# First attention: scores formed twice, the second time keys by queries, with the exponential taken straight from PSUM

## The chip, the cores and the metric

The kernel runs on one core of a Trainium2 chip. The metric is the device time of one execution in microseconds (us), the median of several runs.

## What is computed

A batch of 16 sequences of 256 tokens, 256 wide, passes two transformer-like layers. The change is in the second step, a causal attention of the normed tokens over a context, with 16 heads of 16 channels and a mask over the keys:

```python
scores = jnp.einsum('bhqd,bhkd->bhqk', q, k) * scale
causal = jnp.tril(jnp.ones((Lq, Ls), bool))
full_mask = causal[None, None] & (mask[:, None, None, :] > 0)
scores = jnp.where(full_mask, scores, -jnp.inf)
p = jax.nn.softmax(scores, axis=-1)
return jnp.einsum('bhqk,bhkd->bhqd', p, v)
```

Around it stand the projections of query, key, value and output, each with a bias, and the addition of the result to x. The stages before it (a decaying sum) and after it (experts, time and channel mixing, a second attention, a last projection) are not touched.

## The kernel before

The whole x lies in SBUF. Each stage is a block with one program for each engine; a barrier parts the stages. In `causal_attention` (tiles named `xa_...`) every engine runs through `for b in long_turns(...)`: 16 batches and two turns of drain. The order on each engine is written out by hand and the engines meet at semaphores. The work of a batch is 16 units (query tile `t` of 128 queries, pair of heads), in four steps of four units.

- TensorE: `scores` (L692) multiplies queries by keys. A head pair stands on one quarter of the array's rows (32 of 128), so that eight products go to four PSUM banks from four quarters. `turn_unit` (L704) transposes the f32 probabilities through the full array into `p_p`. `sum_units` (L723) multiplies them by the values, on quarters of the array's columns (128 rows by 32 columns), with a column of ones that gives the sums. Projections (L654, L662) and the transposes of x, o and sums (L647, L732) use the full array. So three shapes of the array occur: full (128x128), row quarters (32x128), column quarters (128x32).
- VectorE: `shift_unit` (L940) reads scores from PSUM, adds the causal and key mask `neg`, writes `sc` and gives the minimum (the scores have their sign turned) to `nmax`. `copy_unit` (L949) copies half of the transposed units out of PSUM.
- ScalarE: `exponentials` (L860) forms `pr` from `sc` with `nmax` as its bias, one instruction for each head; `copy_unit` (L839) copies the other half; it also reads all projections out of PSUM.
- GpSimd: builds `neg` from the mask (L593, L596), `root`, `finish_values`, `add`.

For the first query tile only the first 128 keys are formed (`keys(t)`), for the second all 256.

## Time and profile before

| | |
|---|---|
| median of three runs | 1957.56 us (1953.01 to 1961.42) |
| span of the profiled execution | 1955.9 us |
| this stage, first scores to last addition | 90.9 to 408.2 us |
| TensorE busy over the span | 87% |
| VectorE, ScalarE, GpSimd busy over the span | 62%, 58%, 32% |

The profiled execution is shown with its span alone, 1955.9 us from first to last instruction, 1.7 us below the median. A matmul's row gives its start and a modelled end; rows that follow one another on TensorE overlap by the pipeline's depth, so what a matmul costs is read from start to start.

### The profile page before, as it was taken

Reading aid. Unit: us, or ns where it says so; the run is one execution under the profiler, and the core shown is the slowest. Engines: PE = TensorE matmul, PEld = TensorE weight load, DVE = VectorE, ACT = ScalarE, POOL = GpSimd, SP = SyncE. Lnnn points to the kernel's source line nnn. Section 1 sums busy time; section 2 is a strip of 40 time slices with the busy share of each in tenths; the row PEclk is TensorE's granted clock in tenths of the full one; section 3 lists DMA queues with packets and bytes.
Section 4 is the critical chain, followed back from the end, with each engine's and each line's share of the span. In section 5 each row is a group of like instructions: output and inputs, shape, how many; then the busy total and the mean of one; then the engine's idle time right before and its main releaser. Section 6 shows DMA issues by size and latency. Waiting matters only on the chain. (4 is left out here: it accounts for less than half of the span.)

```text
span 1955.9 us, 40754 instructions
## 1 busy us (share of the span) xinstructions
PE 1699.3 (87%) x13412; PEld 1389.0 (71%) x13412; DVE 1214.7 (62%) x4180; ACT 1133.1 (58%) x2600; POOL 621.2 (32%) x783
## 2 busy tenths in 40 slices
PE   6677777779999999999988999999996999999963
PEld 5555555557788888889976877777774777777742
DVE  6699999858211111101118899899954988888756
ACT  5599999932222222222326665666643888888855
POOL 4523333230211111101114566666622122222217
PEclk9899999979999999999988999999997999999985
DMA  3100010035855556557944000000002111111002
GB/s 119 48 26 26 19 26 18 3 103 187 272 182 182 194 165 205 166 188 243 324 156 150 22 22 23 22 18 16 22 1 73 35 34 34 34 34 35 2 1 86
DMA packets 111695, 171.96 MB, mean 88 GB/s; under 512 B 6832, under 2 KB 86576, under 8 KB 110864
## 3 DMA queue, kind: packets, MB, share of 16 engines
q1 hardware_dynamic: 95248, 142.55, 22.1%
q0 software_dynamic: 6480, 17.70, 3.1%
q10 hardware_dynamic: 9776, 9.31, 1.4%
q8 instruction: 101, 1.65, 0.3%
q14 instruction: 90, 0.74, 0.1%
HBM read 143.45 MB, written 26.08 MB: 87 GB/s over the span
## 5 line engine op out<-in xcount | busy, mean ns | idle before, releaser
L1909 ACT ACTIVATE moe_hT<-moe_p_h,lane_a 128x256 f32<-128x256 f32 (+1 forms) x344 | 131.4, 433 | 370.1 <-PE moe_p_h L1851 370.1
L1851 PE MATMUL moe_p_h<-moe_gT,moe_w 128*128 128x256 f32 (+1 forms) x1376 | 254.0, 343 | 0.8 <-issue 0.8
L1861 PE MATMUL moe_p_y<-moe_w,moe_hT 128*128 128x256 f32 x1136 | 252.3, 379 | 0.0
L1359 ACT ACTIVATE xb_pr<-xb_sc,xb_nmax 128x256 f32<-128x256 f32 x512 | 221.1, 501 | 39.3 <-DVE xb_nmax L1416 39.1
L1851 PEld LDWEIGHTS moe_p_h<-moe_gT,moe_w 128*128 128x128 f32 x1376 | 226.1, 191 | 24.9 <-issue 1.0
L1861 PEld LDWEIGHTS moe_p_y<-moe_w,moe_hT 128*128 128x128 f32 x1136 | 212.5, 190 | 27.1
L1416 DVE CUSTOM_DVE_ANT_0 xb_sc<-xb_p_s,xb_neg 128x256 f32<-128x256 f32 x512 | 187.1, 420 | 54.6 <-PE xb_p_s L1225 53.2
L860 ACT ACTIVATE xa_pr<-xa_sc,xa_nmax 128x256 f32<-128x256 f32 (+1 forms) x512 | 204.1, 453 | 17.6 <-DVE xa_nmax L940 17.1
L1741 POOL DMA_INDIRECT moe_gx<-moe_tokens,moe_source_i x71 | 67.3, 948 | 454.5 <-PE moe_p_t L1838 398.5
L2054 DVE TENSOR_TENSOR moe_gy<-moe_p_y,lane_a 128x256 f32<-128x256 f32 x71 | 27.5, 421 | 229.1 <-PE moe_p_y L1861 229.1
L2029 DVE COPY moe_gT<-moe_p_t 128x512 f32<-128x512 f32 (+1 forms) x43 | 25.7, 598 | 230.2 <-PE moe_p_t L1838 230.2
L1237 PE MATMUL xb_p_p<-ident,xb_pr 128*128 128x128 f32 x1024 | 145.3, 280 | 24.9 <-DVE xb_prT L1425 17.1
L940 DVE CUSTOM_DVE_ANT_0 xa_sc<-xa_p_s,xa_neg 128x256 f32<-128x256 f32 (+1 forms) x512 | 151.6, 352 | 10.7 <-PE xa_p_s L692 9.2
L1237 PEld LDWEIGHTS xb_p_p<-ident,xb_pr 128*128 128x128 f32 x1024 | 112.6, 142 | 52.9 <-ACT xb_pr L1359 27.1
L704 PE MATMUL xa_p_p<-ident,xa_pr 128*128 128x128 f32 x768 | 118.6, 283 | 20.8 <-DVE xa_prT L949 14.9
L2334 PE MATMUL mix_p_kv<-mix_fv,mix_hid_sq 128*128 128x256 f32 x512 | 115.7, 379 | 1.7 <-ACT mix_hid_sq L2543 1.7
L704 PEld LDWEIGHTS xa_p_p<-ident,xa_pr 128*128 128x128 f32 x768 | 84.5, 144 | 44.8 <-ACT xa_pr L860 24.1
L2411 PE MATMUL mix_p_h<-mix_mixed,mix_fk 128*128 128x256 f32 x512 | 114.5, 382 | 0.0
L2411 PEld LDWEIGHTS mix_p_h<-mix_mixed,mix_fk 128*128 128x128 f32 x512 | 98.6, 193 | 13.8
L2334 PEld LDWEIGHTS mix_p_kv<-mix_fv,mix_hid_sq 128*128 128x128 f32 x512 | 96.0, 190 | 14.5 <-ACT mix_hid_sq L2543 2.1
L1425 DVE COPY xb_prT<-xb_p_p 128x512 f32<-128x512 f32 x128 | 87.7, 685 | 1.7 <-PE xb_p_p L1237 1.6
L1341 ACT ACTIVATE xb_prT<-xb_p_p 128x512 f32<-128x512 f32 x128 | 74.8, 584 | 16.0 <-PE xb_p_p L1237 15.9
(344 smaller groups left out, 3447.2 us busy)
## 6 DMA issues: line engine op xcount, KB each, us to landing
moe_w<-in_L_ffn_w_dram SPq DMA_DIRECT2D x86, 1024.0 KB, 8.0
moe_rows_out<-moe_gy ACTq DMA_DIRECT2D x28, 256.0 KB, 7.1
xb_kv<-moe_w SPq DMA_DIRECT2D x18, 256.0 KB, 2.9
X<-in_x_dram SPq DMA_DIRECT2D x4, 1024.0 KB, 9.5
xa_ctx<-in_ctx_turned_dram SPq DMA_DIRECT2D x16, 256.0 KB, 2.8
moe_tokens<-moe_XN_s SPq DMA_DIRECT2D x16, 256.0 KB, 2.2
xb_k_in<-xb_kv SPq DMA_DIRECT2D x16, 256.0 KB, 2.6
xb_v_in<-xb_kv SPq DMA_DIRECT2D x16, 256.0 KB, 3.0
```

Source lines behind the costliest of these rows:

```text
L704: last = pe.transpose(p_p[m % 2][:, (e * TB + kt) * P:(e * TB + kt + 1) * P], pr[:, m % RB, e, kt * P:(kt + 1) * P], ident[:, :])
L860: last = act.activation(pr[:, n % RB, e, 0:width], sc[:, n % RB, e, 0:width], ACT.Exp, bias=nmax[:, n % RB, e:e + 1], scale=-1.0)
L940: last = dve.tensor_tensor_reduce(out=sc[:, n % RB, e, 0:keys(t)], in0=scored_in(n, e), in1=neg[:, s, t, 0:keys(t)], scale=1.0, scalar=3e3 ...
L1237: last = pe.transpose(p_p[m % 2][:, (e * TB + kt) * P:(e * TB + kt + 1) * P], pr[:, m % RB, e, kt * P:(kt + 1) * P], ident[:, :])
L1359: last = act.activation(pr[:, n % RB, e, :], sc[:, n % RB, e, :], ACT.Exp, bias=nmax[:, n % RB, e:e + 1], scale=-1.0)
L1416: last = dve.tensor_tensor_reduce(out=sc[:, n % RB, e, :], in0=scored_in(n, e), in1=neg[:, s, t, :], scale=1.0, scalar=3e38, op0=ALU.add, ...
L1425: dve.tensor_copy(*turned_unit(m)).then_inc(s_["p_copied_v"], 1)
L1851: last = pe.matmul(p_h[n % 3][:, k * width:(k + 1) * width], w1[:, r, ic, (2 * n + k) * P:(2 * n + k + 1) * P], gT[:, r % 2, ic, 0:width], ...
L1861: last = pe.matmul(p_y[:, t * D:(t + 1) * D], hT[:, hc, t * P:(t + 1) * P], w2[:, r, hc, :], start=(hc == 0), stop=(hc == HC - 1))
L1909: last = act.activation(hT[:, 2 * n + k, 0:width], p_h[n % 3][:, k * width:(k + 1) * width], ACT.Gelu, bias=b1[:, bass.ds(e * HC + 2 * n + ...
L2334: last = pe.matmul(p_kv[:, t * D:(t + 1) * D], hid_sq[:, hc, t * P:(t + 1) * P], fv[:, hc, :], start=(hc == 0), stop=(hc == HC - 1))
L2411: last = pe.matmul(p_h[m % 2][:, k * S:(k + 1) * S], fk[:, ic, (2 * m + k) * P:(2 * m + k + 1) * P], mixed2[:, 0, ic, :], start=(ic == 0), ...
```

## The change

The scores are formed twice. In the first pass (`score`, 12 fills of a bank for each batch, f = 0 to 11) queries stand on the partitions; TensorE first adds the mask itself (the identity times `off`, with `OFF` a power of two), then two or four products of row quarters on top of it in the same bank. VectorE only takes the minimum of the bank (`find_max`). GpSimd splits the minima into three bf16 parts that sum to them (`part`), TensorE transposes these (`turn_max`) and ScalarE copies them (`read_max`). In the second pass, one batch later (`cross`, g = 0 to 11), keys stand on the partitions: product of keys and queries, plus a product that adds the three parts of the minima (`pick` by `nmaxT`), plus the identity times `ahead`, the causal triangle. ScalarE takes the exponential of a whole bank of 512 out of PSUM (`exponentials`), with the key mask as its bias. These probabilities are already laid out for `sum_values`: the transposes of `turn_unit` and both copies of `copy_unit` are gone. The key bias of `finish_keys` moves from VectorE to ScalarE, the key mask `mask_keys` from GpSimd to VectorE; a transposed copy of the mask is one more small input.

```diff
-OFF = 1e30
+OFF = 2.0 ** 100
...
+FILLS = 12
+RING_S = 2
+RING_T = 3
+PARTS = 3
+SLOT = 16
...
+            def part(n):
+
+                slots = [parts[:, :, :, SLOT:].rearrange("p t o (u x) -> p t o u x", x=SLOT)[:, :, :, :, i] for i in range(PARTS)]
+                own = nmax[:, n % 2, :, :, :]
+                wait_alone(pool, s_["stood_p"], (s_["maxed"], FILLS * n + FILLS))
+                if n >= 1:
+                    wait_alone(pool, s_["stood_p"], (s_["turned_max"], n))
+                pool.tensor_copy(slots[0], own).then_inc(s_["split"], 1)
+                wait_alone(pool, s_["stood_p"], (s_["split"], 3 * n + 1))
+                pool.tensor_tensor(rest[:, :, :, :], own, slots[0], ALU.subtract).then_inc(s_["split"], 1)
+                wait_alone(pool, s_["stood_p"], (s_["split"], 3 * n + 2))
+                pool.tensor_copy(slots[1], rest[:, :, :, :]).then_inc(s_["split"], 1)
+                wait_alone(pool, s_["stood_p"], (s_["split"], 3 * n + 3))
+                pool.tensor_tensor(slots[2], rest[:, :, :, :], slots[1], ALU.subtract).then_inc(s_["parted"], 1)
...
+            def score(n, f):
+                if f == 0:
+                    pe.wait_ge(s_["q_ready"], n + 1)
+                    pe.wait_ge(s_["k_ready"], n + 1)
+                    pe.wait_ge(s_["diag_ready"], n + 1)
+                if FILLS * n + f >= RING_S:
+                    pe.wait_ge(s_["maxed"], FILLS * n + f - RING_S + 1)
+                bank, view = p_s[f % RING_S], fill_view(f)
+                if f < 8:
+                    c, r = divmod(f, 4)
+                    pe.matmul(view, ident_d[:, :], off[:, n % 2, 1:TB + 1, :].rearrange("p t n -> p (t n)").unsqueeze(1).broadcast_to([P, 2, S]),
+                              start=True, stop=False)
+                    for odd in range(2):
+                        last = pe.matmul(bank[:, odd * S:(odd + 1) * S], q[quad(r), n % 3, odd, c, P:2 * P], k[quad(r), n % 3, c, :],
+                                         start=False, stop=(odd == 1))
+                else:
+                    r = f - 8
+                    pe.matmul(bank[:, :].rearrange("p (m n) -> p m n", m=4), ident_d[:, :], off[:, n % 2, 0:1, :].broadcast_to([P, 4, P]),
+                              start=True, stop=False)
+                    for c in range(DC):
+                        for odd in range(2):
+                            last = pe.matmul(bank[:, (2 * c + odd) * P:(2 * c + odd + 1) * P], q[quad(r), n % 3, odd, c, 0:P], k[quad(r), n % 3, c, 0:P],
+                                             start=False, stop=(c == DC - 1 and odd == 1))
+                last.then_inc(s_["scored"], 1)
+
+            def cross(n, g):
+                if g == 0:
+                    pe.wait_ge(s_["max_ready"], n + 1)
+                if FILLS * n + g >= RING_T:
+                    pe.wait_ge(s_["exped"], FILLS * n + g - RING_T + 1)
+                bank, r = p_x[g % RING_T], g % 4
+                if g < 4:
+                    for c in range(DC):
+                        pe.matmul(bank[:, c * S:(c + 1) * S].rearrange("p (o n) -> p o n", o=2), k[quad(r), n % 3, c, P:2 * P], q[quad(r), n % 3, :, c, P:2 * P],
+                                  start=True, stop=False)
+                        pe.matmul(bank[:, c * S:(c + 1) * S].rearrange("p (o n) -> p o n", o=2), pick[quad(r), c, :], nmaxT[quad(r), :, P:2 * P],
+                                  start=False, stop=False)
+                        last = pe.matmul(bank[:, c * S:(c + 1) * S].rearrange("p (o n) -> p o n", o=2), ident_d[:, :], ahead[:, :].unsqueeze(1).broadcast_to([P, 2, P]),
+                                         start=False, stop=True)
+                else:
+                    c = g // 4 - 1
+                    pe.matmul(bank[:, :].rearrange("p (o n) -> p o n", o=2), k[quad(r), n % 3, c, 0:P], q[quad(r), n % 3, :, c, :], start=True, stop=False)
+                    pe.matmul(bank[:, :].rearrange("p (o n) -> p o n", o=2), pick[quad(r), c, :], nmaxT[quad(r), :, :], start=False, stop=False)
+                    last = pe.matmul(bank[:, :].rearrange("p (o n) -> p o n", o=2)[:, :, 0:P], ident_d[:, :], ahead[:, :].unsqueeze(1).broadcast_to([P, 2, P]),
+                                     start=False, stop=True)
+                last.then_inc(s_["crossed"], 1)
...
+            def sum_values(n, c):
+
+                pe.wait_ge(s_["exped"], FILLS * n + 8 + 4 * c)
+                if c == 0:
+                    pe.wait_ge(s_["v_ready"], n + 1)
+                if n > 0 or c > 0:
+                    pe.wait_ge(s_["sums_read"], DC * n + c)
+                for odd in range(2):
+                    for r in range(4):
+                        pe.matmul(p_o[quad(r), odd * S:(odd + 1) * S], v[:, n % 3, 0, head(c, r, odd), :], pr0[:, c, r, odd, :],
+                                  start=True, stop=False)
+                    for r in range(4):
+                        last = pe.matmul(p_o[quad(r), odd * S + P:(odd + 1) * S], v[:, n % 3, 1, head(c, r, odd), :], pr1[:, r, c, odd, :],
+                                         start=False, stop=True)
+                last.then_inc(s_["pv"], 1)
...
+            def turn_max(n):
+
+                pe.wait_ge(s_["parted"], n + 1)
+                for odd in range(2):
+                    for t in range(TB):
+                        last = pe.transpose(p_d[0][:, odd * S + t * P:odd * S + (t + 1) * P],
+                                            parts[:, t, odd, SLOT - 4 * odd:SLOT - 4 * odd + P], ident_d[:, :])
+                last.then_inc(s_["turned_max"], 1)
...
+            for b in range(B + 2):
+                here, past, old = b < B, 1 <= b <= B, b >= 2
+                if here:
+                    score(b, 0)
+                    score(b, 1)
+                if old:
+                    pe.wait_ge(s_["o_ready"], DC * (b - 2) + 1)
+                    turn_sums(b - 2, 1)
+                if past:
+                    if here:
+                        pe.wait_ge(s_["v_read"], b + 1)
+                    else:
+                        pe.wait_ge(s_["y_read"], B - 2)
+                    turn_max(b - 1)
+                if here:
+                    score(b, 2)
+                if b + 1 < B:
+                    if old:
+                        pe.wait_ge(s_["o_ready"], DC * (b - 1))
+                    else:
+                        pe.wait_ge(s_["q_read"], b + 1)
+                    project_keys(b + 1)
+                if here:
+                    score(b, 3)
+                if past:
+                    cross(b - 1, 0)
+                    cross(b - 1, 1)
...
+            def exponentials(n, g):
+
+                act.wait_ge(s_["crossed"], FILLS * n + g + 1)
+                if n >= 1 and g == 0:
+                    act.wait_ge(s_["pv"], DC * n)
+                if g < 4:
+                    act.activation(pr1[:, g, :, :, :].rearrange("p c o q -> p (c o q)"), p_x[g % RING_T][:, :], ACT.Exp,
+                                   bias=key_bias[:, n, 1:2], scale=-1.0).then_inc(s_["exped"], 1)
+                else:
+                    act.activation(pr0[:, g // 4 - 1, g % 4, :, :].rearrange("p o q -> p (o q)"), p_x[g % RING_T][:, :], ACT.Exp,
+                                   bias=key_bias[:, n, 0:1], scale=-1.0).then_inc(s_["exped"], 1)
...
-            def shift_unit(b, s, n):
-                t = n // PAIRS
-                if n == 0:
-                    dve.wait_ge(s_["neg_ready"], b + 1)
-                    dve.sem_inc(s_["stood_v"], 1)
-                if n >= RB or since(b, 1):
-                    wait_alone(dve, s_["stood_v"], (s_["scored"], UNITS * b + n // STEP * STEP + STEP), (s_["exped"], UNITS * b + n - RB + 1))
+            def find_max(n, f):
+                dve.wait_ge(s_["scored"], FILLS * n + f + 1)
+                if n >= 2 and f == 0:
+                    wait_alone(dve, s_["stood_v"], (s_["parted"], n - 1))
+                if f < 8:
+                    c, r = divmod(f, 4)
+                    out = nmax[:, n % 2, 1, :, 2 * r + c]
                 else:
-                    dve.wait_ge(s_["scored"], UNITS * b + n // STEP * STEP + STEP)
-                for e in range(2):
-                    last = dve.tensor_tensor_reduce(
-                        out=sc[:, n % RB, e, 0:keys(t)], in0=scored_in(n, e), in1=neg[:, s, t, 0:keys(t)], scale=1.0, scalar=3e38,
-                        op0=ALU.add, op1=ALU.min, accum_out=nmax[:, n % RB, e:e + 1])
-                last.then_inc(s_["shifted"], 1)
...
+            def find_max(n, f):
+                dve.wait_ge(s_["scored"], FILLS * n + f + 1)
+                if n >= 2 and f == 0:
+                    wait_alone(dve, s_["stood_v"], (s_["parted"], n - 1))
+                if f < 8:
+                    c, r = divmod(f, 4)
+                    out = nmax[:, n % 2, 1, :, 2 * r + c]
                 else:
-                    dve.wait_ge(s_["scored"], UNITS * b + n // STEP * STEP + STEP)
-                for e in range(2):
-                    last = dve.tensor_tensor_reduce(
-                        out=sc[:, n % RB, e, 0:keys(t)], in0=scored_in(n, e), in1=neg[:, s, t, 0:keys(t)], scale=1.0, scalar=3e38,
-                        op0=ALU.add, op1=ALU.min, accum_out=nmax[:, n % RB, e:e + 1])
-                last.then_inc(s_["shifted"], 1)
-
-            def copy_unit(b, m):
-                dve.wait_ge(s_["p_turned"], UNITS * b + m + 1)
-                if m >= RB or since(b, 1):
-                    dve.wait_ge(s_["pv"], UNITS * b + m - RB + 1)
-                dve.tensor_copy(*turned_unit(m)).then_inc(s_["p_copied_v"], 1)
-
-            def normalise(b, t):
-
-                dve.wait_ge(s_["sums_turned"], TB * b + t + 1)
-                if t == 0 and since(b, 1):
-                    dve.wait_ge(s_["turned_o"], b)
-                heads = p_a[:, 0:H * VW].rearrange("p (h r) -> p h r", r=VW)
-                chain.done(dve.reciprocal(inv[:, t, :], heads[:, :, DH]))
+                    out = nmax[:, n % 2, 0, :, 2 * (f - 8):2 * (f - 8) + 2].rearrange("p o c -> p c o")
+                dve.tensor_reduce(out, fill_view(f), AX.X, ALU.min).then_inc(s_["maxed"], 1)
```

TensorE before, the start of a batch up to the output projection (xa_p_s scores, xa_p_a the bank for projections and transposes, xa_p_p transposed probabilities, xa_p_o sums):

```order
L704 MATMUL xa_p_p<-ident,xa_pr 128x128 x8
L723 MATMUL xa_p_o<-xa_prT,xa_v 32x128 x8
L692 MATMUL xa_p_s<-xa_k,xa_q 128x128 x8
L647 MATMUL xa_p_a<-xa_ident_d,xa_o 128x128 x4
L704 MATMUL xa_p_p<-ident,xa_pr 128x128 x8
L662 MATMUL xa_p_a<-lane_b,xa_oT 128x256 x4
L704 MATMUL xa_p_p<-ident,xa_pr 128x128 x8
L723 MATMUL xa_p_o<-xa_prT,xa_v 32x128 x16
L732 MATMUL xa_p_a<-ident,xa_sums 128x128 x4
L692 MATMUL xa_p_s<-xa_k,xa_q 128x128 x8
```

TensorE now, the middle of a batch: one first-pass fill and two second-pass fills (xa_p_s the banks of the first pass, xa_p_x of the second, xa_p_m of projections and transposes). Rows with xa_off, xa_ahead and the projection use the full array, those with xa_q, xa_k or xa_pick a quarter of its rows:

```order
L686 MATMUL xa_p_s1<-xa_off,xa_ident_d 128x512
L689 MATMUL xa_p_s1<-xa_k,xa_q 128x256 x2
L717 MATMUL xa_p_x1<-xa_q,xa_k 128x512
L718 MATMUL xa_p_x1<-xa_nmaxT,xa_pick 128x512
L719 MATMUL xa_p_x1<-xa_ahead,xa_ident_d 128x2x128
L717 MATMUL xa_p_x2<-xa_q,xa_k 128x512
L718 MATMUL xa_p_x2<-xa_nmaxT,xa_pick 128x512
L719 MATMUL xa_p_x2<-xa_ahead,xa_ident_d 128x2x128
L672 MATMUL xa_p_m0<-lane_b,xa_oT 128x256 x4
L686 MATMUL xa_p_s0<-xa_off,xa_ident_d 128x512
L689 MATMUL xa_p_s0<-xa_k,xa_q 128x256 x2
```

Between two projections the array's shape now changes with nearly every instruction, where before one group of 8 to 32 instructions of one shape followed another. From one L752 to the next, TensorE's order changes shape 46 times in a batch; before, from one output projection to the next, 13 times.

TensorE now, the start of a batch, which holds the waits for VectorE and GpSimd (xa_sums is what ScalarE read of xa_p_o, xa_parts what GpSimd made of the minima):

```order
L686 MATMUL xa_p_s0<-xa_off,xa_ident_d 128x512
L689 MATMUL xa_p_s0<-xa_k,xa_q 128x256 x2
L686 MATMUL xa_p_s1<-xa_off,xa_ident_d 128x512
L689 MATMUL xa_p_s1<-xa_k,xa_q 128x256 x2
L744 MATMUL xa_p_m1<-ident,xa_sums 128x128 x4
L752 MATMUL xa_p_m0<-xa_ident_d,xa_parts 128x128 x4
L686 MATMUL xa_p_s0<-xa_off,xa_ident_d 128x512
L689 MATMUL xa_p_s0<-xa_k,xa_q 128x256 x2
L664 MATMUL xa_p_m1<-xa_cT,lane_b 128x256 x4
```

L744 and L752 are new at this place: the turned sums of the batch before last stand ahead of the turned minima of the last one, and the first cross (xa_p_x0) stands behind both.

## Rows read from the trace of the kernel before

**Rows 1.** Window of one batch: busy us of each engine (x instructions), then granted clock.

```profile
core 0: us, PE busy (x) PEld busy (x) DVE busy (x) ACT busy (x) POOL busy (x), PEclk, DMA share, GB/s
...
242.21:261.39 19.18, 15.08 (x212) 10.40 (x209) 17.73 (x93) 18.22 (x49) 6.35 (x11) 1.00 0.09 23
```

**Rows 2.** Groups by line in that batch: xcount | busy us, mean ns | idle before.

```profile
L860 ACT ACTIVATE xa_pr<-xa_sc,xa_nmax 128x256 f32<-128x256 f32 (+1 forms) x32 | 12.8, 454 | 1.0 <-DVE xa_nmax L940 0.9
L940 DVE CUSTOM_DVE_ANT_0 xa_sc<-xa_p_s,xa_neg 128x128 f32<-128x128 f32 (+1 forms) x32 | 9.5, 353 | 0.5 <-PE xa_p_s L692 0.5
L704 PE MATMUL xa_p_p<-ident,xa_pr 128*128 128x128 f32 x48 | 7.3, 278 | 1.0 <-DVE xa_prT L949 0.7 <-ACT xa_prT L839 0.2
...
L949 DVE COPY xa_prT<-xa_p_p 128x512 f32<-128x512 f32 (+1 forms) x9 | 5.1, 566 | 0.0
```

**Rows 3.** Timeline of TensorE in that batch: start us, us, line, names, array shape, xcount.

```profile
242.21 0.29 PE L692 MATMUL xa_p_s<-xa_k,xa_q 32*128 32x128 bf16 x8
242.43 0.40 PE L647 MATMUL xa_p_a<-xa_ident_d,xa_o 128*128 128x128 bf16 x4
...
246.13 1.08 PE L723 MATMUL xa_p_o<-xa_prT,xa_v 128*32 128x128 f32 x32
247.14 0.66 PE L732 MATMUL xa_p_a<-ident,xa_sums 128*128 128x128 f32 x4
247.73 0.29 PE L692 MATMUL xa_p_s<-xa_k,xa_q 32*128 32x128 bf16 x8
...
251.53 0.40 PE L692 MATMUL xa_p_s<-xa_k,xa_q 32*128 32x256 bf16 x8
251.86 0.40 PE L647 MATMUL xa_p_a<-xa_ident_d,xa_xn 128*128 128x128 bf16 x4
252.09 0.61 PE L704 MATMUL xa_p_p<-ident,xa_pr 128*128 128x128 f32 x4
```

**Rows 4.** Timeline of TensorE, matmuls of 512 bf16 columns, later stage.

```profile
435.21 0.59 PE L1773 MATMUL moe_p_c<-moe_warm 128*128 128x512 bf16 x2
435.64 0.95 PE L1766 MATMUL moe_p_h<-lane_a,moe_xT 128*128 128x8 f32 x8
```

**Rows 5.** Groups by line and shape, whole span: exponentials, copies, the widest reduction.

```profile
L860 ACT ACTIVATE xa_pr<-xa_sc,xa_nmax 128x256 f32<-128x256 f32 x256 | 116.2, 508 | 2.3 <-DVE xa_nmax L940 1.8
...
L860 ACT ACTIVATE xa_pr<-xa_sc,xa_nmax 128x128 f32<-128x128 f32 x256 | 87.9, 398 | 15.3 <-DVE xa_nmax L940 15.3
...
L949 DVE COPY xa_prT<-xa_p_p 128x512 f32<-128x512 f32 x64 | 43.7, 683 | 0.9 <-PE xa_p_p L704 0.8
...
L839 ACT ACTIVATE xa_prT<-xa_p_p 128x512 f32<-128x512 f32 x64 | 37.4, 585 | 0.3 <-PE xa_p_p L704 0.3
...
L1989 DVE TENSOR_REDUCE moe_owner<-moe_passed 128x43 f32<-128x645 f32 x1 | 0.8, 824 | 0.0
```

**Rows 6.** Timeline of GpSimd: small operations.

```profile
246.30 0.19 POOL L83 TENSOR_SCALAR xa_rstd<-xa_aggr 128x2 f32<-128x2 f32 x1
246.68 0.71 POOL L85 TENSOR_TENSOR xa_rstd<-xa_rstd,minus_half 128x2 f32<-128x2 f32 x1 [0.18 <-POOL xa_rstd L83]
```

**Rows 7.** Timeline of VectorE: one call of normalise.

```profile
247.83 0.26 DVE L957 RECIPROCAL xa_inv<-xa_p_a 128x16 f32<-128x16 f32 x1 [0.22 <-PE xa_p_a L732]
248.12 0.49 DVE L961 TENSOR_TENSOR xa_o<-xa_p_a,xa_inv 128x128 bf16<-128x128 f32 x2
```

**Rows 8.** Window of ten us in the first batch, columns as in group 1.

```profile
100.00:110.00 10.00, 8.93 (x83) 6.49 (x80) 8.70 (x45) 9.46 (x24) 2.13 (x4) 0.66 0.01 3
```

**Rows 9.** Timeline: first scores of the first and last batch, last products and addition.

```profile
90.90 0.40 PE L692 MATMUL xa_p_s<-xa_k,xa_q 32*128 32x128 bf16 x8
...
376.63 0.29 PE L692 MATMUL xa_p_s<-xa_k,xa_q 32*128 32x128 bf16 x8
...
400.19 1.08 PE L723 MATMUL xa_p_o<-xa_prT,xa_v 128*32 128x128 f32 x32
...
407.07 1.16 POOL L613 TENSOR_TENSOR X<-xa_y_f,X 128x512 f32<-128x512 bf16 x1 [6.77 <-remote]
```

More of the change, by code:

```diff
@@ L958, in normalise @@
+            def normalise(n, c):
+                dve.wait_ge(s_["sums_turned"], DC * n + c + 1)
+                if c == 0 and n >= 1:
+                    dve.wait_ge(s_["turned_o"], n)
+                heads = p_m[1][:, :].rearrange("p (h r) -> p h r", r=VW)
+                chain.done(dve.reciprocal(inv[:, c, :], heads[:, :, DH]))
                 chain.wait()
-                for c in range(DC):
-                    own = slice(H // DC * c, H // DC * (c + 1))
+                for t in range(TB):
+                    own = slice(H // TB * t, H // TB * (t + 1))
@@ L979, in _ @@
             chain.wait()
+            for c in range(DC):
+                chain.done(dve.tensor_scalar(pick[:, c, :], ones_d[:, :], parity[:, c:c + 1], DH ** 0.5, ALU.mult, ALU.mult))
             chain.done(dve.tensor_copy(cols_d[:, :, :], cols_r[:, :, :]))
```

580 lines of the change are left out of this document (280 added, 300 removed).

## The prediction

> **What bounds the kernel now.** The change stays inside one stage, so I read that stage and not the shares of the whole span. It runs from the first scores at 90.90 to the end of the addition that starts at 407.07 [rows 9], 317.3 us. From the batch at 242.21 [rows 3] to the one at 376.63 [rows 9] lie seven batches of 19.2 us. The window of one batch [rows 1] shows ScalarE busy 18.22 of 19.18 us and VectorE 17.73, TensorE 15.08. The first two set the pace together. The groups [rows 2] say with what: 32 exponentials (12.8 us) and half the copies on ScalarE, 32 shifts (9.5) and the other half of the copies (5.1) on VectorE. TensorE's 15.08 must not be read as work, since each row ends one pipeline's depth after its last column. From start to start [rows 3]: four bf16 products of 128 columns take 0.23 us (251.86 to 252.09), 0.0575 each; two of 512 take 0.43 [rows 4], 0.215 each; so 256 cost 0.108. The f32 groups fit twice the bf16 price per column for each issued instruction, 0.115 for 128 (eight rounds of four in the 1.01 us from 246.13 to 247.14). Real TensorE work in a batch is then 48 transposes at 0.115 = 5.5, about 24 rounds of value products = 2.8, scores 0.7, 16 projection products 1.7, and turns of x, o and sums 1.4: 12.1 us.
>
> **A price the change meets often.** Where the array changes its shape, the rows leave a gap that columns don't explain [rows 3]: 242.21 to 242.43 is 0.22 us for two rounds of 128 columns (0.115), 0.105 left; 251.53 to 251.86 is 0.33 for two rounds of 256 (0.215), 0.115 left; 247.14 to 247.73 leaves 0.13; 246.13 to 247.14 leaves 0.09. From 251.86 to 252.09, without a change of shape, nothing is left. I take 0.10 us a change. Before, 13 changes in a batch are 1.3 us, on an engine that waits anyway. In the new order there are 46.
>
> **Part by part, for one batch in steady state.**
>
> *VectorE.* 32 shifts and 8 copies go, 12 reductions of 512 elements come. The trace has none from PSUM. Nearest rows [rows 5]: a reduction of 645 elements from SBUF 0.82 us, a copy of 512 from PSUM 0.68 with the tail that overlaps the next; I take 0.62 from start to start, between 0.55 and 0.82. 12 of them are 7.4 (to 9.8). What stays of 17.7 us after shifts (9.5) and copies (5.1) is 3.1 and what overlaps them, some 5. New load 12.5, at most 15.
>
> *ScalarE.* 12 exponentials of 512 out of PSUM. Rows of 256 and 128 [rows 5] give 508 and 398 ns, so 0.86 ns an element; 512 give 0.73, some 0.62 from start to start as copies of 585 ns lie; bounds 0.58 and 0.73. 7.4 us. Nine copies at 0.58 (one new, the maxima) are 5.2, the key bias from VectorE under 1. New load 13.5, at most 15.
>
> *GpSimd.* Four small operations in a chain for the three parts. Nearest rows [rows 6]: 0.19 us of work and 0.18 of handing over, upper bound 0.71 of work. Sum 1.5 us, between 1.5 and 3.6.
>
> *TensorE.* The transposes go, 5.5 us. Counting every product of the new order: 28 of 512 columns bf16 (12 key masks, 16 in the second pass) 6.02; 64 of 256 columns (16 in the first pass, 32 in the second, 16 projections) 6.91; 28 of 128 columns bf16 1.61; 8 f32 transposes of sums 0.92; 32 value products, issued as 64 in 16 rounds of four, half of 256 columns, half of 128, 8 x 0.23 + 8 x 0.115 = 2.76. Sum 18.2. The score products, which four row quarters did side by side, now stand alone: a fill has one quarter. Only where a fill ends on one quarter and the next product starts on another (after fills 3, 4, 5, 7, 9) do they overlap, 4 x 0.108 + 0.06 = 0.49 off. 17.7 us of columns, plus 46 x 0.10 = 4.6: 22.3 us in which TensorE never waits. That is above the old batch of 19.18 and above the new loads of 12.5 and 13.5, so TensorE becomes the bound.
>
> The Trainium skill, TensorE: Matmul & The Clock Gate, section Back-to-back issue gap, gives about 131 ns for each matmul of 512 columns in a sustained stream with weight loads. Here the row shows 215 ns [rows 4]. By the page the 28 would cost 3.7 us, not 6.0, the batch 20.2 and the kernel about 1983 us.
>
> *Waits on TensorE.* Its order leaves one tight place, the start of a batch. Two fills take 1.24 us, the turned sums end at 1.7, the turned maxima at 1.9, the third fill at 2.5; then `project_keys` writes the bank that `normalise` reads. VectorE gets the second fill at about 1.35, ends its minimum at 1.95, and `normalise` (0.26 + 0.49 us and a handover [rows 7]) ends at 2.8. TensorE waits 0.3 us. The last minimum of the batch before lands some 0.35 us before this batch begins, as TensorE then sums values for 1.4 us; 1.5 us of GpSimd later is 1.2, before the turned maxima are due at 1.7: hidden, with 0.5 us to spare. Behind that wait everything of both passes is queued. All other hand-overs have over 1 us of other TensorE work between. Batch: 22.3 + 0.3 = 22.6 us.
>
> **The sum.** The first batch took 285.7 - 14 x 19.18 = 17.2 us before [rows 9]. Now it has a first pass and projections, 6.8 us of columns and 2.5 of changes, in a stretch with the clock at 0.66 [rows 8], a mix of 1.2 and 2.4 GHz: 13 at that mean, 16 at 1.2 GHz; I take 14, -3.2 us. The prologue has more constants, but its root no longer stands behind the mask work on GpSimd: 0. The 15 batches after: 15 x (22.6 - 19.18) = +51.3. The drain was 12.4 us (395.8 to 408.2). Now the last batch's second pass runs alone: 3.0 until its maxima are turned and copied, 10.1 for 12 crosses (4 x 1.05, 8 x 0.74), 1.2 for outputs and sums, 3.2 for values, 0.5 of waits, then the old tail of 7.0 from the last value product [rows 9]: 25.0, +12.6. Together +60.7 on 1955.9, the profiled span; the medians should differ alike, 1957.56 + 60.7 = 2018.
>
> **Rivals.**
>
> *A change of shape costs nothing where the next product is ready* (not slower). In all the new order 15 x 46 + 24 + 42 = 756 changes hold 75.6 us of my sum; without them the kernel is 14.9 us faster, 1943. It breaks even where a change costs 0.02 us. Against it: four changes of three kinds all leave 0.09 to 0.13. The Trainium skill, TensorEngine Tiling, Key Properties, says that a change of tiling mode, not of tile, drains the engine; by that every one of the 46 pays. Chance 0.05.
>
> *The maxima come late.* With GpSimd at its upper bound (3.6 us) the parts land at 3.3 instead of 1.7 us. TensorE stands 1.6 us longer with all of both passes behind it, of which the 0.3 us wait is absorbed: 1.3 x 15 is 19.5, and a last reduction of 0.82 us instead of 0.62, with one just like it ahead, adds 0.4 x 15: 2037 to 2044. It decides once the four operations take over 2.0 us. Chance 0.18.
>
> *Columns overlap as in the page's rule*: 1983, chance 0.02; the row of 215 ns is against it.
>
> *VectorE or ScalarE stays the bound*: it needs over 1.4 us a reduction or exponential of 512, against 0.82 and 0.73 at most. Nothing moves then until 20 us. Chance 0.02.
>
> *The gains and losses cancel* (ends, clock and a cheaper change together, within 0.5%): 0.05. The forecast: 0.68.
>
> **Numbers.** The forecast's own spread: changes at 0.09 and no wait give 21.9 a batch, -10.5, first batch 10 instead of 14: 2004. On the other side the late maxima reach 2044. Taking both in leaves out the three cases below 2000, most of the cancelling one and a tail of the forecast, under 2 in 10: range 2001 to 2045. A measurement of this kernel tells about 0.5% (10 us) from no change. Faster by more: 0.05; within: 0.05; slower: 0.90.
>
> **What would show it.** In the new trace: a batch of 22 to 23 us; TensorE with almost no idle in the middle of the stage, start to start of a 512-column mask product and the quarter product behind it 0.31 us (0.215 + 0.10); VectorE and ScalarE idle for over a third; reductions of about 0.65 us; `turn_max` not waiting for `parts`, `project_keys` waiting 0.3 us for `o`. Wrong would be: gaps of shape changes near 0.02, a batch set by a reduction or exponential over 1.2 us, or a wait of over 1 us before the turned maxima.

## The result, and the profile after

The changed kernel takes 2034.09 us (2032.74 to 2035.1, four runs) against 1958.6 us (1953.01 to 1961.42, four runs) for the kernel before: ratio 1.0393, 95% interval 1.0376 to 1.0411. It is slower, inside the range and 16 us above the predicted 2018. The profiled execution spans 2032.7 us, 76.8 more than before. One execution told of below, of 2119.7 us in the unmasked kernel, was in a slow state and is left out of that kernel's figures.

Windows of the kernel after: the first batch, most of the second, one steady batch, the drain. They answer to [rows 1, 8]: busy us of each engine (instructions), then the granted clock as a share of 2.4 GHz. All later windows have the same columns.

```profile
core 0: us, PE busy (x) PEld busy (x) DVE busy (x) ACT busy (x) POOL busy (x), PEclk, DMA share, GB/s
93.34:110.71 17.37, 15.94 (x60) 5.37 (x61) 10.35 (x22) 3.29 (x6) 5.40 (x11) 0.50 0.07 23
110.71:143.00 32.29, 31.62 (x153) 10.34 (x156) 11.51 (x26) 12.62 (x20) 5.55 (x13) 0.55 0.04 13
255.27:277.45 22.18, 21.96 (x196) 10.08 (x193) 12.39 (x31) 13.88 (x23) 6.15 (x13) 1.00 0.07 19
455.00:485.00 30.00, 23.86 (x140) 8.24 (x138) 3.00 (x13) 12.31 (x19) 2.32 (x2) 0.66 0.00 1
```

The steady batch takes 22.18 us instead of 19.18, and TensorE is busy in 21.96 of them; VectorE and ScalarE have fallen from 17.73 and 18.22 to 12.39 and 13.88. The bound has moved as forecast. A batch's length is read from the turned maxima (L752), which begin at 146.12, 168.31, 190.49 and so on to 412.32, then 434.66 and 454.88. The first two batches and the drain are another matter: there the clock column says 0.50, 0.55 and 0.66. In the clock's record TensorE stands at 1.2 GHz from 82.0 to 140.0 us, again from 457.5 to 474.5, and from 481.4 on past the end of the stage at 484.8. That is 67 us of the stage; the kernel before had 17 (to 97.3, 100.7 to 107.5, and from 404.5 on).

Groups by line in the steady batch, which answer to [rows 2]: count | busy us, mean ns | idle before.

```profile
L1023 DVE TENSOR_REDUCE xa_nmax<-xa_p_s 128x2 f32<-128x512 f32 (+1 forms) x12 | 8.1, 689 | 8.7 <-PE xa_p_s L689 7.3 <-PE xa_p_s L697 1.4
L933 ACT ACTIVATE xa_pr<-xa_p_x,xa_key_bias 128x512 f32<-128x512 f32 x8 | 5.5, 687 | 1.3 <-PE xa_p_x L719 1.1
...
L930 ACT ACTIVATE xa_pr<-xa_p_x,xa_key_bias 128x512 f32<-128x512 f32 x4 | 2.7, 682 | 1.0 <-PE xa_p_x L713 1.0
```

A reduction of 512 elements from PSUM takes 0.69 us, an exponential of 512 from PSUM 0.685; both engines idle between them.

Timeline of TensorE from the start of that batch, which answers to [rows 3]: start us, us, line, names, array shape, count.

```profile
254.94 0.40 PE L735 MATMUL xa_p_o<-xa_pr,xa_v 128*32 128x128 f32 x8
255.27 0.39 PE L686 MATMUL xa_p_s<-xa_off,xa_ident_d 128*128 128x512 bf16 x1
255.59 0.39 PE L689 MATMUL xa_p_s<-xa_k,xa_q 32*128 32x256 bf16 x2
255.91 0.39 PE L686 MATMUL xa_p_s<-xa_off,xa_ident_d 128*128 128x512 bf16 x1
256.23 0.39 PE L689 MATMUL xa_p_s<-xa_k,xa_q 32*128 32x256 bf16 x2
256.55 0.66 PE L744 MATMUL xa_p_m<-ident,xa_sums 128*128 128x128 f32 x4
257.05 0.39 PE L752 MATMUL xa_p_m<-xa_ident_d,xa_parts 128*128 128x128 bf16 x4
...
258.18 0.61 PE L664 MATMUL xa_p_m<-xa_cT,lane_b 128*128 128x256 bf16 x4 [0.22 <-DVE xa_o L1035]
...
258.94 0.28 PE L689 MATMUL xa_p_s<-xa_k,xa_q 32*128 32x256 bf16 x1
258.95 0.28 PE L709 MATMUL xa_p_x<-xa_q,xa_k 32*128 32x256 bf16 x1
```

From start to start: the mask product of 512 columns and the quarter product behind it, 0.32 us (255.27 to 255.59), 0.215 columns and 0.105 change; the two quarter products back to the full array, 0.32 again. The value products on column quarters, two rounds of 128 columns (0.23) from 254.94 to 255.27, leave 0.10. The turned sums (L744) and turned maxima (L752) follow without a wait. The only wait is 0.22 us before `project_keys` (L664), for VectorE's `o`. The rows at 258.94 and 258.95 start together: they stand on different quarters.

Later in the same batch, a fill and the crosses behind it, same columns:

```profile
266.27 0.39 PE L689 MATMUL xa_p_s<-xa_k,xa_q 32*128 32x256 bf16 x2
266.50 0.37 PE L717 MATMUL xa_p_x<-xa_q,xa_k 32*128 32x512 bf16 x1
266.72 0.37 PE L718 MATMUL xa_p_x<-xa_nmaxT,xa_pick 32*128 32x512 bf16 x1
267.02 0.28 PE L719 MATMUL xa_p_x<-xa_ahead,xa_ident_d 128*128 128x256 bf16 x1
267.24 0.38 PE L717 MATMUL xa_p_x<-xa_q,xa_k 32*128 32x512 bf16 x1
```

From 266.27 to 266.50, quarter to quarter, 0.23 us for 256 columns twice: nothing is left but some 0.012 us, which products of one shape on one row quarter show elsewhere too. 266.72 to 267.02 is 0.30 for 512 columns (0.085 left), 267.02 to 267.24 is 0.22 for 256 (0.11 left).

The same cross at 1.2 GHz, in the drain:

```profile
462.31 0.60 PE L717 MATMUL xa_p_x<-xa_q,xa_k 32*128 32x512 bf16 x1
462.71 0.63 PE L718 MATMUL xa_p_x<-xa_nmaxT,xa_pick 32*128 32x512 bf16 x1
463.27 0.39 PE L719 MATMUL xa_p_x<-xa_ahead,xa_ident_d 128*128 128x256 bf16 x1
463.60 0.60 PE L717 MATMUL xa_p_x<-xa_q,xa_k 32*128 32x512 bf16 x1
```

One cross of 1280 columns takes 1.29 us (462.31 to 463.60) instead of 0.74 (266.50 to 267.24). If its columns take twice the 0.54 us that they take at 2.4 GHz, 0.22 are left for two changes of shape: by this estimate a change costs about 0.11 us at 1.2 GHz too, and hardly grows as the columns do.

Timeline of GpSimd, the four operations of `part`; [rows 6] had stood for them:

```profile
254.99 0.32 POOL L590 CAST xa_parts<-xa_nmax 128x32 bf16<-128x32 f32 x1 [1.00 <-DVE xa_nmax L1023]
255.49 0.27 POOL L592 TENSOR_TENSOR xa_rest<-xa_nmax,xa_parts 128x32 f32<-128x32 f32 x1 [0.18 <-POOL xa_parts L590]
255.92 0.32 POOL L594 CAST xa_parts<-xa_rest 128x32 bf16<-128x32 f32 x1 [0.17 <-POOL xa_rest L592]
256.42 0.33 POOL L596 TENSOR_TENSOR xa_parts<-xa_rest,xa_parts 128x32 bf16<-128x32 f32 x1 [0.18 <-POOL xa_parts L594]
```

From 254.99 to the end at 256.75 the chain takes 1.76 us, more than the 1.5 of the sum, and ends 0.3 us before the turned maxima begin at 257.05. One batch shows the edge: from 432.45 it takes 2.07 us (the third operation starts 0.46 us after the end of the second instead of 0.17), the turned maxima wait, and from the maxima before to these it is 22.34 us.

### The profile page after: what moved, and what is told of

The parts are those of the page before. It is cut to its first block and busy times, and to the rows that moved or that the text cites. A ratio compares the mean times of both kernels' runs of the same rounds, so it can differ in the third digit from the quotient of the medians.

```text
span 2032.7 us, 37939 instructions
## 1 busy us (share of the span) xinstructions
PE 1838.2 (90%) x13151; PEld 1389.6 (68%) x13156; DVE 1128.6 (56%) x3207; ACT 1063.7 (52%) x2200; POOL 616.9 (30%) x819
## 5 line engine op out<-in xcount | busy, mean ns | idle before, releaser
L1023 DVE TENSOR_REDUCE xa_nmax<-xa_p_s 128x2 f32<-128x512 f32 (+1 forms) x192 | 129.8, 689 | 149.8 <-PE xa_p_s L689 122.6
L2138 DVE TENSOR_TENSOR moe_gy<-moe_p_y,lane_a 128x256 f32<-128x256 f32 x71 | 27.5, 420 | 229.4 <-PE moe_p_y L1945 229.4
L2495 PEld LDWEIGHTS mix_p_h<-mix_mixed,mix_fk 128*128 128x128 f32 x512 | 98.0, 191 | 13.6
L933 ACT ACTIVATE xa_pr<-xa_p_x,xa_key_bias 128x512 f32<-128x512 f32 x128 | 87.9, 687 | 29.5 <-PE xa_p_x L719 25.7
L1425 ACT ACTIVATE xb_prT<-xb_p_p 128x512 f32<-128x512 f32 x128 | 74.8, 584 | 16.0 <-PE xb_p_p L1321 15.9
L1309 PE MATMUL xb_p_s<-xb_k,xb_q 32*128 32x256 f32 x1024 | 75.2, 408 | 6.4 <-DVE xb_nmax L1500 4.3
L2330 POOL DMA_INDIRECT mix_got<-moe_rows_out,mix_which x64 | 69.0, 1078 | 28.1 <-issue 15.8
```

Of the source, the lines that this page charges most:

```text
L933: act.activation(pr0[:, g // 4 - 1, g % 4, :, :].rearrange("p o q -> p (o q)"), p_x[g % RING_T][:, :], ACT.Exp, bias=key_bias[:, n, 0:1], ...
L1023: dve.tensor_reduce(out, fill_view(f), AX.X, ALU.min).then_inc(s_["maxed"], 1)
L1309: last = pe.matmul(p_s[r][:, odd * S:(odd + 1) * S], q[VW * r:VW * (r + 1), s, odd, c, t * P:(t + 1) * P], k[VW * r:VW * (r + 1), s, c, :] ...
L2495: last = pe.matmul(p_h[m % 2][:, k * S:(k + 1) * S], fk[:, ic, (2 * m + k) * P:(2 * m + k + 1) * P], mixed2[:, 0, ic, :], start=(ic == 0), ...
```

## The experiments

Each ratio is against the kernel before, run beside it on the same chip; its medians there were 1954.8 to 1958.9 us.

### Shape by shape

`triple` issues a fill of the first pass with the two crosses that follow it so that products of one shape stand together. The columns stay the same; the changes of shape fall from 46 to 26 a batch. This tests the dearest disputed term, together with the overlap of products that come to stand side by side.

```diff
-                if here:
-                    score(b, 3)
-                if past:
-                    cross(b - 1, 0)
-                    cross(b - 1, 1)
+                triple(b, 3, 0)
...
+                if n < B:
+                    open_fill(n, f)
...
+                    for x in pair:
+                        cross_full(n - 1, x)
+                if n < B:
+                    add_scores(n, f)
+                for x in pair:
+                    cross_quads(n - 1, x)
```

> Same products and columns as the changed kernel, but each first-pass fill and its two second-pass fills are issued shape by shape: full-array products together, row-quarter products together. Changes of the array's shape in a batch: 26 instead of 46. Theory (TensorE is the bound, a change of shape costs 0.095 us): 20 changes give 1.9 us, and neighbours on different row quarters, which now follow one another, overlap for another 1.1 us; batch 19.2 instead of 22.18 us, kernel about 1985. Rival (a change costs nothing, only columns count): batch 21.1, kernel 2017. Rival (a wait or another engine sets the pace): no change, 2034.

Measured: 2018.07 us, 1.0295 (1.0267 to 1.0324). Windows of two batches that follow one another, same columns as above:

```profile
178.35:198.40 20.05, 17.88 (x190) 9.26 (x188) 12.96 (x32) 13.30 (x23) 6.17 (x12) 1.00 0.07 20
198.40:224.28 25.88, 23.92 (x191) 11.02 (x188) 12.42 (x32) 13.45 (x23) 6.16 (x12) 0.74 0.07 17
```

The first of them, at 2.4 GHz, is 2.13 us shorter than in the changed kernel, with 20 changes fewer; 19.2 us had been expected, and 1985 for the kernel. Timeline of TensorE in it:

```profile
180.69 0.28 PE L696 MATMUL xa_p_s<-xa_k,xa_q 32*128 32x256 bf16 x1
180.69 0.29 PE L721 MATMUL xa_p_x<-xa_q,xa_k 32*128 32x256 bf16 x2
180.81 0.27 PE L696 MATMUL xa_p_s<-xa_k,xa_q 32*128 32x256 bf16 x1
180.81 0.28 PE L722 MATMUL xa_p_x<-xa_nmaxT,xa_pick 32*128 32x256 bf16 x2
180.92 0.28 PE L721 MATMUL xa_p_x<-xa_q,xa_k 32*128 32x256 bf16 x2
181.03 0.28 PE L722 MATMUL xa_p_x<-xa_nmaxT,xa_pick 32*128 32x256 bf16 x2
181.25 0.40 PE L657 MATMUL xa_p_m<-xa_ident_d,xa_o 128*128 128x128 bf16 x4
...
182.40 0.59 PE L733 MATMUL xa_p_x<-xa_ahead,xa_ident_d 128*128 128x512 bf16 x2 [0.54 <-ACT xa_pr L941]
...
184.74 0.40 PE L657 MATMUL xa_p_m<-xa_ident_d,xa_xn 128*128 128x128 bf16 x4 [1.19 <-DVE xa_xn L91]
```

The rows from 180.69 are products of two crosses and of the fill, on different quarters, and they run side by side: ten of 256 columns in the 0.56 us to 181.25, a change of shape among them, where one after another they would be 1.08 (10 x 0.108). The expectation had 1.1 us a batch for this. In exchange TensorE now waits 0.54 us for an exponential and 1.19 us for the normed x. The second window is the surprise: 25.88 us for the same work, with the clock at 0.74. The batches repeat as 20.05, 20.05, 25.8, 22.8 us to the end of the stage. The median lies at the 2017 of the rival in which changes cost nothing, but by chance: that rival had 21.1 us for every batch. So the batch does get shorter where shapes are grouped, and part of what is saved there is given back by the clock.

### The cover of the other engines

Two edits on the changed kernel, one for each chain that might set the batch. In the first, `find_max` reads half of each fill (its minima are those of half the keys). In the second, GpSimd makes one part instead of three (the maxima are rounded to bf16, and slots 1 and 2 keep what they held).

```diff
-                dve.tensor_reduce(out, fill_view(f), AX.X, ALU.min).then_inc(s_["maxed"], 1)
+                dve.tensor_reduce(out, fill_view(f)[:, :, 0:P] if f < 8 else fill_view(f)[:, :, :, 0:P // 2], AX.X, ALU.min).then_inc(s_["maxed"], 1)
```

```diff
-                pool.tensor_copy(slots[0], own).then_inc(s_["split"], 1)
...
-                pool.tensor_tensor(slots[2], rest[:, :, :, :], slots[1], ALU.subtract).then_inc(s_["parted"], 1)
+                pool.tensor_copy(slots[0], own).then_inc(s_["parted"], 1)
```

> The reductions read half of each bank, 256 elements instead of 512; the maxima leave out half of the keys. Theory (VectorE is not the bound and the last minimum is not late): no change, 2034 within 5 us. Rival (VectorE or the late maxima hold TensorE): 12 reductions fall from 0.62 to 0.35 us, up to 3.2 us a batch and up to 50 us in all.

> GpSimd makes one bf16 part of the maxima instead of three; the second and third part are left out, so the chain before the turned maxima is one operation instead of four. Theory (the chain is hidden behind the value products and two fills): no change in steady batches, at most 3 us in all from the first and last batch. Rival (the maxima come late): up to 1 us a batch, 15 us.

Measured: 2039.09 us, 1.0408 (1.0382 to 1.0434), steady batch 22.08; and 2031.73 us, 1.037 (1.0348 to 1.0392), steady batch 22.19. Neither moves the steady batch by more than 0.1 us: the reductions and the chain of the maxima are hidden. The first is even 5 us above the changed kernel, though the two intervals overlap; its trace has the clock at 1.2 GHz from 439.7 to 460.2 us and a last batch of 28.98 us, where the changed kernel's is 20.22. The work got less and the time did not. Windows of the first kernel, ahead of that fall and behind it:

```profile
417.60:439.70 22.10, 22.10 (x191) 9.71 (x187) 8.33 (x25) 12.85 (x22) 4.31 (x8) 1.00 0.00 1
439.70:460.20 20.50, 20.50 (x119) 7.51 (x117) 3.70 (x11) 6.52 (x10) 2.41 (x5) 0.50 0.00 1
```

TensorE did not wait once in the 22.10 us before the clock fell, nor in the 20.50 us after it; the gaps of shape changes count as busy here.

### Dummy products ahead of and in the first batch

The second batch took 33.6 us, nearly all of it at 1.2 GHz. One theory: TensorE's waits in the prologue had brought the clock down. The first edit puts 25 products of 512 columns there, whose result nobody reads; the second adds one more behind each fill of the first batch.

```diff
+            def keep_busy(n):
+                for i in range(n):
+                    pe.matmul(p_x[i % RING_T][:, :], ident_d[:, :], w[:, 0, :, :].rearrange("p c d -> p (c d)"), start=True, stop=True)
+
+            keep_busy(8)
```

```diff
+                    keep_busy(1 if b == 0 else 0)
```

> 25 products of 512 columns, whose results nobody reads, fill TensorE's waits before the first batch (8 before the first projection, 12, 2 and 3 between the others). In the changed kernel the granted clock is 0.50 from 82 to 140 us although TensorE is over 90% busy from 93 on. Theory (the stretch at 1.2 GHz costs the first batch and most of the second double columns; it began with TensorE's idle prologue): with the engine busy there the clock stays or returns early, the second batch falls from 33.6 to about 22 us and the first from 17.4 to about 12; 2034 becomes 2018. Rival (the clock falls for another reason, or the extra products only delay): same or up to 3 us slower.

> As the kernel that kept TensorE busy before the first batch, and one more product of 512 columns that nobody reads behind each of the 12 fills of the first batch, where the clock fell again at 98 us. Theory (what is over the forecast, 17.4 and 33.6 us for the first two batches instead of 14 and 22.6, is the clock at 1.2 GHz): with 2.4 GHz held through the first batch, that takes 12 and the second 22.2: 2034 becomes 2018. If the clock falls all the same, the extra products cost up to 3 us at 1.2 GHz and the kernel is at 2031 or above.

Measured: 2031.23 us, 1.0377 (1.0354 to 1.04), and 2030.46 us, 1.0376 (1.0354 to 1.0399). In both the clock came to 2.4 GHz near the start of the first batch, at 91.1 and 93.1 us, and fell inside it again, at 97.9 and 99.9 us, until 135.4 and 137.4; from turned maxima to turned maxima the second batch took 31.7 us in both, instead of 32.5. The expected 2018 did not come: what holds the clock down there is not the prologue's waits alone. Near the second fall TensorE still waited for the normed x, 1.82 and 1.38 us, which neither edit filled; behind it, from 99.90 to 137.40 in the second kernel, it was busy 36.93 of 37.50 us and stayed at 1.2 GHz. The 3 us between the medians are not clear of the noise, as both intervals overlap that of the changed kernel, and the stage ends at 484.1 and 486.0 us against 484.8.

### The mask left out of the first pass

An upper bound of the maxima is enough for a softmax, so the first pass need not see the mask (the second pass still does). That takes away 12 products of 512 columns and five changes of shape, 3.1 us by the terms of the forecast. It was tried in the changed kernel's order and on top of the grouped order.

```diff
-                    pe.matmul(view, ident_d[:, :], off[:, n % 2, 1:TB + 1, :].rearrange("p t n -> p (t n)").unsqueeze(1).broadcast_to([P, 2, S]),
-                              start=True, stop=False)
...
-                                         start=False, stop=(odd == 1))
+                                         start=True, stop=True)
```

> The changed kernel without the mask in its first pass: the 12 products of 512 columns with the identity are left out, so the maxima are taken over all keys, masked ones too, which is an upper bound of the true maximum and leaves the softmax the same. Per batch 12 x 0.215 us of columns and 5 changes of shape less, 46 to 41. Theory (TensorE is the bound): 22.18 - 2.58 - 0.48 = 19.1 us a batch, kernel 2034 - 16 x 3.05 = about 1985 if the clock stays at 2.4 GHz; as the grouped order showed stretches at 1.2 GHz in steady batches, some such stretches may add up to 3 us a batch. Rival (another engine sets the pace): batch stays at 22.

> Grouped order and no mask in the first pass (maxima over all keys, as an upper bound). 21 changes of shape. TensorE without waits: the grouped order's batch of 20.05 had about 2.1 us of waits, so 17.9, less 2.58 and 0.5: 14.8 us; VectorE and ScalarE, busy some 12.5 and 13.4 us a batch, then come near, so 15.5 to 16.5 us a batch at 2.4 GHz, kernel 2034 - 16 x 6 = about 1938, under the kernel before (1958). If the clock falls more often because TensorE waits more, up to 1975.

Measured: 2054.95 us (median of three), 1.0488 (1.0438 to 1.0538), and 2029.94 us, 1.0375 (1.035 to 1.04). Expected were about 1985, and 1938 to 1975. Less work, and 21 us slower than the changed kernel in the first case, 12 us slower than the grouped one in the second. Windows of the first (at 1.2 GHz, then at 2.4), then of the second:

```profile
194.00:214.50 20.50, 20.23 (x129) 8.58 (x129) 7.13 (x17) 8.29 (x13) 4.85 (x9) 0.50 0.00 1
214.50:235.00 20.50, 19.05 (x183) 8.97 (x182) 13.70 (x35) 13.76 (x23) 6.14 (x12) 1.00 0.07 21
```

```profile
247.10:257.10 10.00, 7.04 (x91) 3.84 (x89) 7.08 (x19) 6.15 (x11) 4.52 (x11) 1.00 0.13 38
257.20:270.80 13.60, 13.10 (x86) 5.65 (x87) 5.37 (x13) 7.15 (x13) 1.46 (x2) 0.50 0.01 3
```

In the first kernel a stretch of 20.4 us at 1.2 GHz comes every 48 to 68 us; its batches are 20.0 to 20.6 us (19.1 expected), and 27.5 where such a stretch falls into them. In the second every batch, 23.89 us, holds 13.6 us at 1.2 GHz. TensorE, with less to do, waits: in the first kernel 0.9 us for the parts of the maxima; in the second 1.2 us for the normed x, 1.0 us for an exponential, 0.5 each for the sums and the parts of the maxima, and its 7.04 busy us of 10 come just ahead of the fall.

### The waits filled

Two theories for the falling clock: (A) it falls because TensorE idles; (B) it falls with the kind of work, for row-quarter products use a quarter of the array. The first edit puts five full-array products of 512 columns, unread, into the 1.2 us in which the grouped kernel waits for the normed x. The second does the same on 32 rows of the array.

```diff
-                pe.wait_ge(s_["normed"], n + 1)
...
+                for i in range(5):
+                    pe.matmul(p_m[1][:, :], ident_d[:, :], w[:, 0, :, :].rearrange("p c d -> p (c d)"), start=True, stop=True)
+                pe.wait_ge(s_["normed"], n + 1)
```

```diff
-                    pe.matmul(p_m[1][:, :], ident_d[:, :], w[:, 0, :, :].rearrange("p c d -> p (c d)"), start=True, stop=True)
+                    pe.matmul(p_m[1][:, :], ident_d[0:VW, :], w[0:VW, 0, :, :].rearrange("p c d -> p (c d)"), start=True, stop=True)
```

> The grouped order with five products of 512 columns that nobody reads in its longest wait (1.2 us, for the normed x before its turn). In the grouped order the clock fell to 1.2 GHz in steady batches: three batches in five take 22.8 or 25.8 us instead of 20.05. Theory A (the fall comes with TensorE's new idle time): it stays at 2.4 GHz, all batches 20.05, kernel about 1985. Theory B (it comes with the larger share of row-quarter products, of which the array does little at a time): batches at 1.2 GHz stay, kernel 2010 to 2020. Full-array products also raise the share of the full array, so a steady clock speaks for either A or this, while a falling clock speaks against A.

> The same five filling products in the same wait of the grouped order as before, but on one row quarter (32 of 128 rows) instead of the full array; nobody reads them. TensorE is busy for the same time. If what keeps the clock at 2.4 GHz is that TensorE doesn't idle: as the full-array fill, all steady batches 20.05 us, kernel 1979. If the kind of product counts: stretches at 1.2 GHz and batches of 22.8 and 25.9 us come back, kernel 2005 to 2020.

Measured: 1979.02 us, 1.0119 (1.01 to 1.0139), and 1983.57 us, 1.013 (1.0111 to 1.015). Window of a batch of the first, then the filled wait in its timeline (the last three of the five products):

```profile
174.15:194.20 20.05, 18.91 (x195) 9.66 (x194) 12.96 (x32) 13.29 (x23) 6.15 (x12) 1.00 0.07 20
```

```profile
179.72 0.81 PE L797 MATMUL xa_p_m<-lane_b,xa_ident_d 128*128 128x512 bf16 x3
180.53 0.40 PE L657 MATMUL xa_p_m<-xa_ident_d,xa_xn 128*128 128x128 bf16 x4
```

Every steady batch is 20.05 us at clock 1.00, in both kernels, and the record has no stretch at 1.2 GHz between 117 and 416 us. Useless work, in a place where TensorE waited anyway, saves 39 us between the medians, 35 when each is taken against the kernel before beside it. In this kernel, then, filling the wait brings the clock back, as (A) has it, and the filling need not use the full array. But (A) does not hold over all the kernels. Window and a wait of the kernel before:

```profile
107.50:404.50 297.00, 230.91 (x3216) 160.02 (x3214) 266.71 (x1377) 276.34 (x727) 92.00 (x144) 1.00 0.07 18
```

```profile
259.13 0.61 PE L662 MATMUL xa_p_a<-lane_b,xa_cT 128*128 128x256 bf16 x4 [1.45 <-DVE xa_o L961]
```

It waits 4.1 us in a batch, 1.45 us of them at once, where the grouped kernel waits 2.2 and 1.19, and it kept 2.4 GHz for all these 297 us. And the kernel with half the reductions fell without any wait (417.60 to 439.70). So TensorE's waits are neither enough for a fall nor needed for one. What part the kind of work has, (B), stays open: only products added in a wait were tried, and the order of the others stayed as it was.

### Both together

The unmasked, grouped kernel with its waits filled (five, two and four products), and the same with x of the next batch measured by VectorE a batch earlier, one part of the maxima, and eight fills.

```diff
+                if b + 2 < B:
+                    measure(b + 2)
```

> Grouped order, no mask in the first pass (maxima over all keys), and TensorE's waits filled with full-array products that nobody reads: 2 before the turned sums, 4 before the second pair of crosses, 5 before the turn of x. The unfilled one spent 13.6 us of each 23.9 us batch at 1.2 GHz. Theory (the clock took the gain): at 2.4 GHz the batch is 23.9 less about half of the columns and changes streamed in those 13.6 us, 16.5 to 17.5, kernel 2034 - 16 x 5.2 = about 1950, from 1940 to 1960. If the fill does not hold the clock: 2010 to 2030.

> As the filled unmasked one, and the two waits themselves shortened: the sums for the norm of the next x are taken at the end of the batch before, so that the turn of x waits for nothing, and GpSimd makes one part of the maxima instead of three (the maxima rounded to bf16; a common shift leaves the softmax the same). Two fill products instead of five at the turn of x. Batch 15.5 to 16.5 us at 2.4 GHz (ScalarE needs 13.4), kernel 1930 to 1950 and under the kernel before. If the clock falls because less is left of full-array work: stretches at 1.2 GHz, 1960 or above.

Measured: 1969.14 us, 1.0058 (1.0034 to 1.0083), and 1967.81 us, 1.005 (1.0034 to 1.0067). Batches of 18.77 and 18.92 us at full clock: less than the 19.18 of before, but more than the 16.5 to 17.5 and 15.5 to 16.5 expected, and so are the times (1940 to 1960, and 1930 to 1950). Window and waits of TensorE in a batch of the second:

```profile
300.30:319.22 18.92, 16.27 (x186) 8.47 (x184) 12.94 (x32) 13.30 (x23) 5.26 (x9) 1.00 0.09 22
```

```profile
301.77 0.61 PE L658 MATMUL xa_p_m<-xa_cT,lane_b 128*128 128x256 bf16 x4 [0.77 <-DVE xa_o L1041]
...
307.01 0.40 PE L651 MATMUL xa_p_m<-xa_ident_d,xa_xn 128*128 128x128 bf16 x4 [0.65 <-DVE xa_xn L91]
...
309.24 0.26 PE L683 MATMUL xa_p_s<-xa_k,xa_q 32*128 32x256 bf16 x1 [0.33 <-ACT xa_pr L939]
...
311.13 0.26 PE L683 MATMUL xa_p_s<-xa_k,xa_q 32*128 32x256 bf16 x1 [0.32 <-ACT xa_pr L939]
...
316.50 0.64 PE L753 MATMUL xa_p_o<-xa_pr,xa_v 128*32 128x256 f32 x8 [0.47 <-ACT xa_pr L939]
```

No engine is full: TensorE 16.27, ScalarE 13.30, VectorE 12.94 of 18.92. The batch is held by hand-overs in both directions, 2.5 us in five places: for `o` and the normed x on VectorE's side, for the ring of three banks on ScalarE's; and the eight fills (1.7 us at 0.215) cost time where a wait is shorter than they are, which no run measured. What 15 batches win, 0.26 or 0.41 us each, the first batches and the drain lose again. No kernel that was run is faster than the kernel before.

## Why the prediction was right, step by step

**TensorE becomes the bound: right.** It is busy 21.96 of 22.18 us; halving the reductions and cutting the chain of the maxima moved the batch by 0.1 at most.

**A change of shape costs 0.10 us: right.** The gaps are 0.085 to 0.11 us in the rows shown. Taking 20 of 46 away shortened a full-clock batch by 2.13 us, in which new waits (1.7 us) and products that now run side by side have their part too; those were not separated, so the price rests on the gaps in the rows. The rival in which changes are free (1943 us) is out. The gap shows where the next product was ready and the shape differed, and is absent between products of one shape. The Trainium skill, TensorEngine Tiling (Array Packing), section Key Properties, says that changing the tiling mode, and not just the tile, drains TensorE; this trace agrees, with 0.085 to 0.11 us against 0.012 at most. The Trainium skill, TensorE: Matmul & The Clock Gate, section Back-to-back issue gap, gives some 131 ns for each matmul of 512 columns in a sustained stream. This trace does not agree: 266.50 to 266.72 is 0.22 us for 512.

**Prices on the other engines: right in effect.** Exponentials of 0.685 us lie inside the bounds of 0.58 to 0.73, reductions of 0.69 inside 0.55 to 0.82. Load of ScalarE 13.88 (13.5 forecast), of VectorE 12.39 (12.5).

**The maxima are hidden: right, by less than I had.** The chain took 1.76 us where the sum had 1.5, still short of the rival's point of 2.0; the one batch in which it took 2.07 became 0.16 us longer. One part instead of three moved no other batch.

**A wait of 0.3 us at `project_keys`: right**, 0.22.

**The batch, 22.6 forecast, 22.18 measured**: over the fourteen batches from 144.3 to 454.9 us that is 5.8 us less than the sum had.

**First batch, second batch and drain: size too small.** The step that missed is the clock. I took 14 us for the first batch, between a mean clock of 0.66 and 1.2 GHz, and the steady 22.6 for the second. Measured were 17.4 (93.34 to 110.71) and 33.6 (to 144.3), both nearly all at 1.2 GHz, +3.4 and +11.0 (1.4 of the 3.4 are a wait for the normed x, which the sum did not have); and the drain, from the last turned maxima at 454.9 to the end of the last addition at 484.8, has 20.4 us at 1.2 GHz and is 29.9 instead of 25.0, +4.9. The stage also began 2.4 us later than before (93.34 against 90.90), of which 1.7 lay ahead of its first instruction. Sum: 2.4 + 3.4 + 11.0 - 5.8 + 4.9 = 15.9 on the forecast's 60.7, 76.6 in all, and the spans differ by 76.8. I had priced columns in the second batch at 2.4 GHz because the kernel before had reached it by 107.5 us; I asked of the clock only where it stood, not whether the new order would let it rise as early.

**What was luck.** The upper end of the range, 2045, stood there for maxima that come late, and they did not. It had no room for a second batch or a drain at 1.2 GHz, which brought some 16 us, and the steady batches gave 5.8 back. The time lies inside for another reason than the range was drawn for.

**What stays open.** Why the clock stayed at 1.2 GHz to 140 us, while TensorE was busy in 31.6 of 32.3 us. Dummy work ahead of and in the first batch hardly changed it (135.4 and 137.4); the grouped kernels with the mask rose at 116.6 to 119.3 us. The order of the products matters, then, but through what is not shown.

## What to carry to other kernels

Count the changes of array shape in a new TensorE order and price each from a gap of the trace: 46 of them at 0.10 us were more than a fifth of this batch. The columns alone, 17.7 us by the forecast's count, would have made TensorE the engine with the most to do, but in less than the old 19.18. Before a saving of TensorE work is trusted, look at the granted clock of several batches in a row, for work taken away can cost the clock. Where it falls, try products that nobody reads in the longest wait; here that helped in one order, while the kernel before kept its clock with longer waits unfilled. Price the first batches and the drain at the clock that they will have, not at that of the steady state.
